# Twelve instead of eight of sixteen key-block pairs in split precision in the last stage of a four-layer graph network

## The reference

```python
x = _layernorm(x + _L0_gnn_ref(x, adj, ...))     # degrees, adj @ x, a 128x128 product
x = _layernorm(x + _L1_gnn_ref(x, adj, ...))     # three products with adj, width 20
x = _layernorm(x + _L2_gnn_ref(x, adj, W, b))    # scaled adj @ (x W + b)
def _L3_gnn_ref(H, adj, W_l, W_r, W_h, W_g, gamma):
    H_l = H @ W_l
    H_r = H @ W_r
    S = H_l @ H_r.T                              # 4096 x 4096
    beta = jax.nn.softmax(S, axis=-1)
    B = beta @ H
    O = B @ W_h @ W_g
    return adj @ H + gamma * O
x = _layernorm(x + _L3_gnn_ref(x, adj, ...))
```

## Time and profile before

| | us |
|---|---|
| median of three runs | 1315.18 |
| the profiled execution | 1312.35 |
| its span, first to last instruction | 1310.1 |
| PE busy | 1258.5 |
| DVE busy | 958.3 |
| ACT busy | 800.8 |
| POOL busy | 242.7 |

### The profile page before, as it was taken

How to read it: one execution, slowest core, us unless ns; L and a number is a source line. 1 busy time by engine, 2 the same in 40 slices (tenths; PEclk the granted TensorE clock), 3 DMA queues, 4 the chain that set the end, 5 groups by cost and what they waited for, 6 DMA issues and landing times.

```text
span 1310.1 us, 17884 instructions
## 1 busy us (share of the span) xinstructions
PE 1258.5 (96%) x6139; PEld 830.1 (63%) x6139; DVE 958.3 (73%) x1266; ACT 800.8 (61%) x966; POOL 242.7 (19%) x143
## 2 busy tenths in 40 slices
PE   8999999989999899999999999998999999999987
PEld 3566666643332334788888888886677776767754
DVE  7987987620000557899999888968878888878885
ACT  1334555511110224888888777767988778788795
POOL 0100000000000000001010000005334333354355
PEclk9999999989999999999999999999999999999998
DMA  9878766689999699899999999950000000000000
GB/s 366 316 266 305 280 246 236 210 328 346 368 342 409 246 394 395 310 384 371 370 387 362 365 362 386 354 210 1 1 1 1 1 1 1 1 19 14 1 1 32
DMA packets 82816, 294.33 MB, mean 225 GB/s; under 512 B 9658, under 2 KB 11322, under 8 KB 82746
## 3 DMA queue, kind: packets, MB, share of 16 engines
q1 hardware_dynamic: 80496, 292.59, 59.5%
q10 hardware_dynamic: 2250, 0.82, 0.3%
HBM read 291.27 MB, written 2.10 MB: 224 GB/s over the span
## 4 chain that ended last, share of the span: by engine, by line
PE 75%; DVE 11%; ACT 6%; issue 4%; DMA 3%; POOL 0%; DVEq 0%; SPq 0%; ACTq 0%
PE acc L1612 8%; PE acc L1607 8%; PE acc L1608 8%; PE acc L1546 7%; PE acc L1460 6%; PE acc L1694 4%; DVE peak L1224 3%; PE acc L1452 3%; DMA raw<-in_adj_s 3%; PE acc L1456 3%; PE acc L1453 3%; ACT ring L912 2%; DVE ring L1246 2%; PE rs L1469 2%; PE rs L1551 2%
## 5 line engine op out<-in xcount | busy, mean ns | idle before, releaser
L1168 DVE TENSOR_TENSOR t_lo<-raw,t_hi 128x1024 fp32r<-128x1024 f32 x256 | 303.9, 1231 | 24.0 <-ACT t_hi L857 18.3
L857 ACT ACTIVATE t_hi<-raw 128x1024 fp32r<-128x1024 f32 x256 | 261.6, 1055 | 40.3 <-PE acc L1612 39.3
L1607 PE MATMUL acc<-t_hi,st_hi 128*128 128x512 f32 x512 | 201.9, 394 | 0.6 <-ACT t_hi L857 0.6
L1608 PE MATMUL acc<-t_hi,st_lo 128*128 128x512 f32 x512 | 199.6, 390 | 0.0
L690 POOL TENSOR_TENSOR ring_lo<-ring,p_hi 128x1024 fp32r<-128x1024 f32 x64 | 155.6, 2431 | 218.2 <-ACT p_hi L906 218.1
L1612 PE MATMUL acc<-t_lo,st_hi 128*128 128x512 f32 x512 | 158.9, 391 | 1.4 <-DVE t_lo L1168 1.1
L1246 DVE TENSOR_TENSOR ring<-ring,e 128x1024 f32<-128x1024 f32 x128 | 154.0, 1211 | 0.1
L900 ACT ACTIVATE ring<-ring 128x1024 f32<-128x1024 f32 x128 | 134.2, 1054 | 26.0 <-DVE ring L1246 25.9
L640 POOL COPY xb<-x 128x512 f32<-128x512 f32 (+1 forms) x24 | 32.3, 1347 | 588.2 <-DVE xs L1086 215.3
L1694 PE MATMUL acc<-ring,x 128*128 128x512 f32 x256 | 120.4, 592 | 0.0
L1612 PEld LDWEIGHTS acc<-t_lo,st_hi 128*128 128x128 f32 x512 | 95.0, 188 | 24.6 <-DVE t_lo L1168 5.0
(11 more groups left out here) (229 smaller groups left out, 2188.4 us busy)
## 6 DMA issues: line engine op xcount, KB each, us to landing
raw<-in_adj_s SPq DMA_DIRECT2D x518, 512.0 KB, 5.6
kept_t<-in_adj_s SPq DMA_DIRECT2D x8, 512.0 KB, 7.0
x<-in_x SPq DMA_DIRECT2D x4, 512.0 KB, 8.3
kept_l<-in_adj_s SPq DMA_DIRECT2D x4, 512.0 KB, 6.7
kept_s<-in_adj_s SPq DMA_DIRECT2D x4, 512.0 KB, 6.7
kept_v<-in_adj_s SPq DMA_DIRECT2D x4, 512.0 KB, 6.7
kept_e<-in_adj_s SPq DMA_DIRECT2D x4, 512.0 KB, 8.5
kept_late<-in_adj_s SPq DMA_DIRECT2D x4, 512.0 KB, 11.3
```

Source lines behind the costliest of these rows:

```text
L857: nc.scalar.activation(t_hi[:, g % HL, :], raw[:, k, :], ACT.Copy).then_inc(hi_done, 1)
L1168: nc.vector.tensor_tensor(t_lo[:, k, :], raw[:, slot_no(s, c, g), :], t_hi[:, k, :].bitcast(F32), ALU.subtract).then_inc(lo_done, 1)
L1607: mm(a[:, :], block_of(st_h, b), hi[:, m], start=(g == 0 and j == 0), stop=False)
L1608: mm(a[:, :], block_of(st_l, b), hi[:, m], start=False, stop=False)
```

## The change

Three of four pairs (k modulo 4 not 0) are split instead of every second: 12 of 16 for each query block, 96 in all instead of 64. The remainders of the values are no longer written to v_lo but over x itself, pair by pair, through a second name for the same memory, x_lo_v. p_hi has three buffers instead of two, and ACT waits for the product of the third last split pair instead of the second last before it overwrites one.

```diff
-SPLIT = tuple(range(1, KP, 2))
+SPLIT = tuple(k for k in range(KP) if k % 4)
+NPH = 3
 NSPLIT = len(SPLIT)
...
+        with ExitStack() as last:
+            x_lo_v = sb("x_lo_v", [P, NB * D], F32R, last)
         x = sb("x", [P, NB * D])
...
-            p_hi = sb("p_hi", [P, 2, PW], F32R, att)
+            p_hi = sb("p_hi", [P, NPH, PW], F32R, att)
             v_hi = sb("v_hi", [P, NSPLIT, 2 * D], F32R, att)
-            v_lo = sb("v_lo", [P, NSPLIT, 2 * D], F32R, att)
...
-                nc.gpsimd.tensor_tensor(ring_lo[:, n % RING, :], slot(n), p_hi[:, m % 2, :].bitcast(F32),
+                nc.gpsimd.tensor_tensor(ring_lo[:, n % RING, :], slot(n), p_hi[:, m % NPH, :].bitcast(F32),
                                         ALU.subtract).then_inc(pl_done, 1)
...
-                    if m > 1:
-                        act.wait_ge(pv_mm, split_pair(m - 2) + 1)
-                    nc.scalar.activation(p_hi[:, m % 2, :], slot(n), ACT.Copy).then_inc(ph_done, 1)
+                    if m >= NPH:
+                        act.wait_ge(pv_mm, split_pair(m - NPH) + 1)
+                    nc.scalar.activation(p_hi[:, m % NPH, :], slot(n), ACT.Copy).then_inc(ph_done, 1)
...
-                nc.vector.tensor_tensor(v_lo[:, j, :], x[:, 2 * k * D:2 * (k + 1) * D],
+                nc.vector.tensor_tensor(cols(x_lo_v, k, 2 * D), x[:, 2 * k * D:2 * (k + 1) * D],
                                         v_hi[:, j, :].bitcast(F32), ALU.subtract).then_inc(vl_done, 1)
...
-                        vh, ph = block_of(v_hi[:, j, :], u), p_hi[:, m % 2, u * CW:(u + 1) * CW]
+                        vh, ph = block_of(v_hi[:, j, :], u), p_hi[:, m % NPH, u * CW:(u + 1) * CW]
                         mm(o, vh, ph, start=(k == 0 and u == 0), stop=False)
-                        mm(o, block_of(v_lo[:, j, :], u), ph, start=False, stop=False)
+                        mm(o, block_of(x_lo_v, 2 * k + u), ph, start=False, stop=False)
```

## The result

The changed kernel takes 1340.64 us (median of 4 runs, 1339.4 to 1342.08), the kernel before beside it 1315.81 (1310.0 to 1317.97): 1.0209 times as long, 95% interval 1.0188 to 1.0229. I had said 1335. The profiled execution took 1339.4 us, its span 1337.6. Lines that I name are the changed kernel's, two above those of before (the copy into mv_all is L1277, the fold L1231, the rounding L908), GpSimd's subtraction L692.

A forecast was written before the change was run, and what follows sets the result against it. PE was taken to bound only half of each period, DVE and ACT the half up to the fold; 1.6 + 11.0 + 3.5 + 5.9 = 22.0 us on 1312.35 gave 1334.4, stated as 1335, range 1318 to 1343.

The forecast's parts named there:

- The copy into mv_all, 2.1 us a period: At k = 9 DVE's statistics copy waits behind POOL's new subtraction, which starts 0.10 us earlier: +2.1 us a period.
- Rival B: DVE's copy into mv_all gets in ahead of POOL, so a period costs only 0.1 us; total 1322, chance 0.20.
- ACT +0.45, PE -0.36: Per period, the new rounding at k = 13 adds 0.45 us; PE's split product at k = 3 saves 0.36.
- Rival C: PE bounds throughout, so its 11.5 us saving counts in full: 1301 us, chance 0.05.
- The first query block, +1.6 from one k = 7 copy to the next: Extra value roundings, remainders and new roundings make the fold 2.0 us later, less 0.36 at k = 3: +1.6 us.
- The last scored ticks, +3.5: Ticks t = 120 to 127: blocked copy 2.1, unhidden rounding at t = 125 1.12, scales 0.3; sum +3.5 us.
- The drain, +5.9: Ticks t = 128 to 148: POOL has 15 subtractions instead of 10, nearly back to back, delaying bt's copy 5.9 us.
- PE's new idle time costs no clock: Some 4 us of PE idle time at each fold was to leave the clock at 1.00.
- Nothing for the rooms and the third buffer: Remainders written over x and the third rounding buffer were to add or remove no waits: 0 us.
- The signs: Expected: L1275 about 2.3 us, periods about 52.7, drain subtractions back to back, busy time PE -11.5, ACT +36, POOL +77 us.

The follow-up runs named there:

- one_6: Changed kernel with only the odd k and k = 6 split, one new pair per query block; 1331.1 us, 1.0132 of the kernel before.
- a_direct: Changed kernel with bn_aggr writing straight into mv_all, so VectorE's copy is gone; 1320.63 us, 1.0061 of the kernel before.
- fill_direct: a_direct plus 14 unread products that TensorE makes before waiting for the sixth folded peak; 1320.28 us, 1.0063 of the kernel before.
- one_10: Changed kernel with only the odd k and k = 10 split, one new pair per query block; 1321.2 us, 1.0055 of the kernel before.
- mem_only: Changed kernel with only the odd k split, so no new split pairs, rooms and buffers kept; 1314.9 us, 1.0005 of the kernel before.
- nph2: Changed kernel with p_hi going round two of its three buffers; 1352.83 us, 1.0291 of the kernel before.
- drain_odd: Changed kernel with pairs from n = 107 on split only where n is odd; 1333.58 us, 1.0154 of the kernel before.
- p_mod2: Changed kernel with the plain pairs moved from k = 0, 4, 8, 12 to k = 2, 6, 10, 14; 1330.51 us, 1.0135 of the kernel before.
- one_14: Changed kernel with only the odd k and k = 14 split, one new pair per query block; 1312.2 us, 0.9985 of the kernel before.

## Why the prediction was right or wrong

- **The copy into mv_all, 2.1 us a period.** Right, cause and size: 2.15 by one_6, 2.35 by taking the copy away. The doubtful point, a lead of 0.10 us, came out at 0.10 in the trace and decided the same way each time. Rival B is refuted.
- **ACT +0.45, PE -0.36.** Right: 0.43 and 0.36, each alone. The regular period was to rise by 2.2 and rose by 2.29. Rival C is refuted: TensorE's saving at k = 7, 11 and 15 is lost.
- **The first query block, +1.6 from one k = 7 copy to the next.** From the copy at 892.45 to that at 979.09 it was 86.64 us and is 88.32 now (892.12 to 980.44): +1.68. Right.
- **The last scored ticks, +3.5.** From the k = 7 copy to the last fold it is +3.23. Right; the halved clock ahead of the fold is not on the chain that ends last.
- **The drain, +5.9: wrong, +10.1.** GpSimd's count was right, as a_direct shows: with all 15 subtractions and no copy the drain is 42.08, +6.0. The step that failed is taking that count as the only thing there. I had priced the blocked copy at one subtraction of GpSimd's in the periods and at nothing in the drain, though the drain is where GpSimd works without a gap; the earlier trace rows showed a copy that got in after one of two. It waited for the rest of four, GpSimd then for its own inputs (3.41 us). Of the 4.1 us between a_direct and the changed kernel this is the greater part and not all. fill_direct, without the copy but with the clock at 0.50 behind the last fold and 4.28 us for the sum into xf, as in the changed kernel, has 42.45, which leaves 3.7; and from GpSimd's last subtraction to bt's copy it is 1.4 us instead of a_direct's 0.8, with the clock at 0.50 again. That leaves about 3.1 for the block, an estimate from these differences; one_10's drain, 39.58 with a copy of 7.82 us, is of the same size.
- **"PE's new idle time costs no clock": wrong.** At the regular folds PE idles 1.27 us ahead of the transposes (2.5 in the whole period, not the 4 that I had named) and keeps its clock. But the table load already left 2.73 us idle at the sixth fold, the change made it 3.81, and the clock fell: 1.6 us (fill_direct). It also fell ahead of the last fold, behind 1.89 us of idle time, and twice in the drain, which is counted above. I had taken the one row of a partly busy stretch for the whole stage.
- **Nothing for the rooms and the third buffer.** Right: mem_only 1.0005; nph2 shows that two buffers would have cost 12.2 us more.
- **The signs.** L1277 at 2.32 us and periods of 52.82 came as said. PE's busy time did not fall by 11.5, and POOL's subtractions in the drain were not all back to back.

The two wrong terms, 4.2 (10.1 less 5.9) and 1.6, are the 5.8 us between the 22.0 that I had summed up and the 27.8 by which bt's last copy moved (28.1 less the 0.3 of the earlier first fold). The 5.6 us between 1335 and 1340.64 look like the same gap, but partly by chance: I had added 22.0 to the profiled 1312.35, and not to the median. From median to median the change is 24.8 us, from profiled execution to profiled execution 27.05.

## What to carry to other kernels

Before giving GpSimd more large SBUF operations, list VectorE's copies between SBUF tensors, however small, and its sums with both inputs in SBUF, and ask for each which GpSimd instruction may be running when it starts; where a copy meets one, let the producer write to the destination, which here took 20 us off. Price such a copy in a stretch in which GpSimd has no gaps by the length of the whole run of instructions, not by one. Split pairs or other added work go where the engine that they relieve is the one that ends last, each position costed by itself: a new pair at k = 6, 10 or 14 was worth +2.15, +0.43 or -0.36 us. Before a drain or a stretch that is some 1.5 us longer in one profile is put down to a wait, look at the granted clock in it: in mem_only and drain_odd the clock was the whole difference.

## What the runs showed of the hardware

**How long a blocked copy waits.** It got in at the end of a GpSimd subtraction, but not always of the first one: of two back-to-back, after the first; in mem_only, of three from 1287.37 on, after the second; in the changed kernel at the end of four; in p_mod2 at the end of five, after 10.11 us:

```profile
1289.01 3.14 DVE L1277 COPY mv_all<-mv_a 128x8 f32<-128x8 f32 x1
...
1287.37 7.17 POOL L692 TENSOR_TENSOR ring_lo<-ring,p_hi 128x1024 fp32r<-128x1024 f32 x3
```

```profile
1299.31 10.11 DVE L1277 COPY mv_all<-mv_a 128x8 f32<-128x8 f32 x1
...
1297.68 11.71 POOL L692 TENSOR_TENSOR ring_lo<-ring,p_hi 128x1024 fp32r<-128x1024 f32 x5
```

The Trainium skill (SBUF — State Buffer, Who interferes with whom) says that whoever starts first holds the shared ports to its end; the traces agree for one instruction, and show that the waiting engine may then lose further turns. What decides at which boundary it gets in is open.

**The clock after idle time.** I took TensorE's idle time ahead of each folded peak from the 16 profiles of the table and looked at the clock in the 3 us behind it. It was at 0.50 there after 12 of 12 idle times of 2.83 us or more, after 5 of 13 between 2.39 and 2.73, after 5 of 14 of 1.94 to 1.96, and after none of the 32 between 1.26 and 1.73. Equal idle times with different outcomes (2.62 us in one_14 and in mem_only) leave open what else decides. A halved stretch cost 1.2 to 1.7 us where it was 3.4 us long and 2.4 to 2.8 where it was 6 to 7. The clock fell at other places too: 19 us ahead of the last fold in the changed kernel and 4 us ahead of it in a_direct, behind idle times of 1.89 and 2.50 us.
